# Four graph layers and an attention over one adjacency matrix: constants on another queue, the sixth sweep streamed and split, a third pair of score banks, and the last root by logarithm and exponential

## What is computed

```python
def ln(x): return (x - mean(x)) / sqrt(var(x) + 1e-5)          # over the 128 columns

# layer 0
inv_deg = 1 / (adj.sum(1) + beta)
x = ln(x + inv_deg[:, None] * (adj @ x + beta[:, None] * x) @ kernel + bias)
# layer 1: three products with adj, the first two 20 columns wide
h = relu(adj @ (x @ W1) + b1); h = relu(adj @ (h @ W2) + b2); h = relu(adj @ (h @ W3) + b3)
x = ln(x + relu(h + x))
# layer 2
d = 1 / (sqrt(adj.sum(1)) + 1e-8)
x = ln(x + (adj * d[:, None] * d[None, :]) @ (x @ W + b))
# layer 3: a product with adj, and an attention over all rows
B = softmax((x @ W_l) @ (x @ W_r).T) @ x
x = ln(x + adj @ x + gamma * (B @ W_h @ W_g))
```

## Time and profile before

| | us |
|---|---|
| median of 3 runs | 1466.33 (1464.1 to 1467.71) |
| the profiled execution | 1466.62 |
| its span, first to last instruction | 1464.8 |
| TensorE, VectorE, ScalarE, GpSimd busy in it | 1380.5, 900.9, 694.5, 235.7 |
| mean granted clock of TensorE | 0.994 |

### The profile page before, as it was taken

One profiled execution on the slowest core, in us unless ns is written; L12 is line 12 of the kernel. 1 busy time (PEld: TensorE's weight loads), 2 busy tenths in 40 slices (PEclk: granted clock), 3 DMA queues, 4 the chain that ended last, 5 costly groups with the idle time before them and its releaser, 6 DMA issues.

```text
span 1464.8 us, 17014 instructions
## 1 busy us (share of the span) xinstructions
PE 1380.5 (94%) x5831; PEld 789.8 (54%) x5831; DVE 900.9 (61%) x1223; ACT 694.5 (47%) x875; POOL 235.7 (16%) x136
## 2 busy tenths in 40 slices
PE   6999999988898899999999999999799999999995
PEld 2555555312122222257777777777567667767753
DVE  3676777300000022488888977776888888888875
ACT  1101011101010111176777866665687878788776
POOL 0111111000000000000101000002033334333343
PEclk9999999999999999999999999999999999999998
DMA  9876677799999999998989889883000000000001
GB/s 345 321 274 230 249 279 266 294 409 407 407 408 408 408 395 397 395 328 312 317 313 324 296 278 327 317 314 129 0 1 1 0 1 1 1 1 1 1 1 58
DMA packets 101151, 337.30 MB, mean 230 GB/s; under 512 B 11354, under 2 KB 12890, under 8 KB 101082
## 3 DMA queue, kind: packets, MB, share of 16 engines
q1 hardware_dynamic: 101082, 336.40, 61.5%
HBM read 334.26 MB, written 2.10 MB: 230 GB/s over the span
## 4 chain that ended last, share of the span: by engine, by line
PE 65%; DMA 13%; DVE 11%; ACT 5%; issue 3%; SPq 2%; POOL 0%; DVEq 0%; ACTq 0%
DMA raw<-in_adj_s 13%; PE acc L1076 11%; PE acc L1112 9%; PE acc L1173 6%; PE acc L1168 6%; PE acc L1169 6%; PE acc L1096 4%; PE acc L1196 4%; DVE peak L861 4%; PE acc L1261 3%; DVE ring L885 3%; ACT ring L615 2%; ACT ring L603 2%; DVE t_lo L794 2%; PE e L989 1%
## 5 line engine op out<-in xcount | busy, mean ns | idle before, releaser
L794 DVE TENSOR_TENSOR t_lo<-raw,t_hi 128x1024 fp32r<-128x1024 f32 x224 | 275.3, 1251 | 61.1 <-ACT t_hi L554 56.8
L554 ACT ACTIVATE t_hi<-raw 128x1024 fp32r<-128x1024 f32 x224 | 234.1, 1058 | 72.7 <-PE acc L1173 71.2
L1168 PE MATMUL acc<-t_hi,st_hi 128*128 128x512 f32 x448 | 201.7, 450 | 2.9 <-DVE st_lo L699 2.9
L475 POOL TENSOR_TENSOR ring_lo<-ring,p_hi 128x1024 fp32r<-128x1024 f32 x64 | 155.5, 2429 | 271.3 <-ACT p_hi L609 271.3
L1076 PE MATMUL acc<-raw,x 128*128 128x512 f32 x384 | 173.3, 606 | 14.6 <-DMA raw<-in_adj_s 14.6
L1112 PE MATMUL acc<-raw,h_a 128*20 128x512 f32 x736 | 162.5, 598 | 22.8 <-DMA raw<-in_adj_s 22.6
L1169 PE MATMUL acc<-t_hi,st_lo 128*128 128x512 f32 x448 | 175.3, 391 | 0.0
L725 DVE TENSOR_TENSOR xs<-e,bias 128x512 f32<-128x512 f32 x8 | 5.5, 690 | 267.0 <-PE e L992 267.0
L499 ACT ACTIVATE at<-acc 128x512 f32<-128x512 f32 x48 | 28.7, 597 | 289.4 <-PE acc L1112 180.9
L885 DVE TENSOR_TENSOR ring<-ring,e 128x1024 f32<-128x1024 f32 x128 | 154.2, 1210 | 0.1
L603 ACT ACTIVATE ring<-ring 128x1024 f32<-128x1024 f32 x128 | 134.7, 1054 | 36.9 <-DVE ring L885 36.8
(11 more groups left out here) (182 smaller groups left out, 2099.1 us busy)
## 6 DMA issues: line engine op xcount, KB each, us to landing
raw<-in_adj_s SPq DMA_DIRECT2D x584, 512.0 KB, 7.3
resident<-in_adj_s SPq DMA_DIRECT2D x16, 512.0 KB, 7.4
raw<-in_adj_s SPq DMA_DIRECT2D x24, 256.0 KB, 7.7
kept_t<-in_adj_s SPq DMA_DIRECT2D x8, 512.0 KB, 5.9
x<-in_x SPq DMA_DIRECT2D x4, 512.0 KB, 8.1
kept_s<-in_adj_s SPq DMA_DIRECT2D x8, 256.0 KB, 6.1
kept_v<-in_adj_s SPq DMA_DIRECT2D x8, 256.0 KB, 6.4
kept_l<-in_adj_s SPq DMA_DIRECT2D x8, 256.0 KB, 9.0
```

Of the source, the lines that this page charges most:

```text
L475: nc.gpsimd.tensor_tensor(ring_lo[:, n % RING, :], slot(n), p_hi[:, m % 2, :].bitcast(F32), ALU.subtract).then_inc(pl_done, 1)
L554: nc.scalar.activation(t_hi[:, (par * NS + g) % HL, :], raw[:, k, :], ACT.Copy).then_inc(hi_done, 1)
L794: nc.vector.tensor_tensor(t_lo[:, k, :], raw[:, slot_no(s, c, g), :], t_hi[:, k, :].bitcast(F32), ALU.subtract).then_inc(lo_done, 1)
L1168: mm(a[:, :], block_of(st_hi, b), hi[:, m], start=(b == 0), stop=False)
```

## The change

- *Constants.* The 18 loads leave SP's queue. ScalarE issues them once the last part of x is in, ahead of its copies of x.
- *Sweep 6* streams all 16 tiles, in 8 slots, and splits all; the resident blocks are not used in it. Its chunk ends are signalled by `pe_tile`.
- *Score banks.* The two accumulators become one tensor `acc01`, which serves as a third pair for the first 15 score steps.
- *Keys and added one.* `k_lo` goes from VectorE to GpSimd; from the fourth key chunk on, each is followed by one of the four additions. The split of the values is five steps later.
- *Peak row.* The four tensor_scalar and the f32 product give way to four transposes with `m4` broadcast as the stationary side.
- *Projection.* The row sums come first, with a semaphore of their own. VectorE's work for group 6 is seven steps later.
- *Last normalisation* in three parts. Blocks 0 to 15 and 16 to 23: variances, root and scales at steps 93 to 95 and 123 to 125, the norms on GpSimd behind its low parts. Blocks 24 to 31 after the last group, five on VectorE and three on ScalarE. The root and reciprocal are exp(-0.5 ln(v)).

```diff
-        LN_PARTS = ((0, NB - CB), (NB - CB, NB))
-        ACT_LN = {NT + 9: (0, 4), NT + 11: (4, 8), NT + 13: (8, 12), NT + 15: (12, 16)}
-        DVE_LN = {NT + 9: (16, 19), NT + 11: (19, 22), NT + 13: (22, 25), NT + 15: (25, 28)}
-        RESULT = ((0, 8, 1), (16, 22, 0), (8, 16, 1), (22, 28, 0), (28, 32, 0))
+        LN_PARTS = ((0, 16), (16, 24), (24, NB))
+        LN_SCALES = (NT - 34, NT - 4)
+        POOL_LN = {NT - 53: (0, 3), NT - 51: (3, 6), NT - 49: (6, 9), NT - 47: (9, 12), NT - 45: (12, 14), NT - 43: (14, 16),
+                   NT - 15: (16, 18), NT - 13: (18, 20), NT - 11: (20, 22), NT - 9: (22, 24)}
+        LN_LAST = (NB - 2 * CB, NB - 3, NB)
+        RESULT = ((0, 9, "fin_xp", 1), (9, 16, "fin_xp", 2), (16, 24, "fin_xp", 3), LN_LAST[:2] + ("fin_x", 1),
+                  LN_LAST[1:] + ("fin_xa", 1))
+        def score_bank(t):
+            return (rs01, e23, acc01)[t % 3] if t < KP - 1 else (e23, rs01)[t % 2]
...
@@ sync
-                        if g == RAW:
-                            for dst, src in consts:
-                                sp.dma_start(dst[:, :], src).then_inc(const_in, 16)
@@ gpsimd
+            def keys_lo(c):
+                pool.wait_ge(k_hi_done, c + 1)
+                nc.gpsimd.tensor_tensor(cols(k_lo, c - 1), cols(v, c), cols(k_hi, c - 1).bitcast(F32),
+                                        ALU.subtract).then_inc(k_lo_done, 1)
+            def normalise_first(a, b):
+                pool.wait_ge(fin_nmr, 1 if b <= LN_PARTS[0][1] else 2)
+                for n in range(a, b):
+                    i = nc.gpsimd.tensor_scalar(block_of(v, n), block_of(xf, n), rstd_a[:, n:n + 1],
+                                                nmr_a[:, n:n + 1], ALU.mult, ALU.add)
...
-            add_one()
+            pool.wait_ge(pe_tile, tile_no(S5, NC - 1, NG - 1) + 1)
+            pool.wait_ge(S["xb"], done("xb", 5, NC - 1))
+            for c in range(1, NC):
+                keys_lo(c)
+                if c >= NC // 2:
+                    add_one(c - NC // 2)
             for n in range(NT):
                 if n % KP in SPLIT:
                     weights_lo(n)
+                if n in POOL_LN:
+                    normalise_first(*POOL_LN[n])
@@ scalar
+            act.wait_ge(x_in[XP - 1], 16)
+            for dst, src in consts:
+                nc.scalar.dma_start(dst[:, :], src).then_inc(const_in, 16)
...
-                nc.scalar.activation(std_a[:, a:b], ve_a[:, a:b], ACT.Sqrt).then_inc(fin_std, 1)
+                nc.scalar.activation(std_a[:, a:b], ve_a[:, a:b], ACT.Ln).then_inc(fin_std, 1)
+                act.wait_ge(fin_std, part + 1)
+                nc.scalar.activation(rstd_a[:, a:b], std_a[:, a:b], ACT.Exp, scale=-0.5).then_inc(fin_rc, 1)
@@ vector
-                dve.wait_ge(m4_done, i + 1)
-                for b in range(CB):
-                    n = nc.vector.tensor_scalar(block_of(diag, b), ident[:, :], m4[:, b:b + 1], None, ALU.mult)
-                n.then_inc(diag_done, 1)
...
-                if i is not None and after == 2:
+                later = 7 if i == GQ - 2 else 0
+                if i is not None and after == 2 + later:
                     finish_sums(i)
@@ tensor
-                for g in range(NS):
-                    hi, lo = t_hi[:, (par * NS + g) % HL, :], t_lo[:, (par * NS + g) % HL, :]
+                for g in range(wide_tiles(s)):
+                    k = (par * wide_tiles(s) + g) % HL
+                    hi, lo = t_hi[:, k, :], t_lo[:, k, :]
...
+                    if s == S5:
+                        continue
                     if g in KEPT_AFTER and not first(c):
...
-                mm(free_banks[i % 2][:, :], ones_f[:, :], diag[:, :], start=True, stop=True).then_inc(row_mm, 1)
+                for b in range(CB):
+                    n = mm(block_of(free_banks[i % 2], b), m4[:, b:b + 1].broadcast_to([P, P]), ident[:, :],
+                           is_transpose=True, start=True, stop=True)
+                n.then_inc(row_mm, 1)
```

More of the change, by code:

```diff
@@ L29 @@
 NS = NG - RB // GB
+S4, S5 = 4, 5
 NT_N = 12
@@ L36 @@
 RAW = 8
-RAW_W = 7
+RAW_4 = 7
 HL = 4
@@ L406, in _ @@
             chunks(sp, step)
-            for n, (a, b, by_act) in enumerate(RESULT):
-                if by_act:
-                    sp.wait_ge(fin_xa, sum(r[2] for r in RESULT[:n]) + 1)
-                else:
-                    sp.wait_ge(fin_x, sum(not r[2] for r in RESULT[:n]) + 1)
+            for a, b, by, count in RESULT:
+                sp.wait_ge({"fin_x": fin_x, "fin_xa": fin_xa, "fin_xp": fin_xp}[by], count)
                 sp.dma_start(out[:, a * D:b * D], v[:, a * D:b * D]).then_inc(out_done, 16)
@@ L925, in last_scales @@
                 a, b = LN_PARTS[part]
-                dve.wait_ge(fin_std, part + 1)
-                nc.vector.reciprocal(rstd_a[:, a:b], std_a[:, a:b]).then_inc(fin_rc, 1)
                 dve.wait_ge(fin_rc, part + 1)
```

158 lines of the change are left out of this document (84 added, 74 removed).

## The result

The changed kernel takes 1441.47 us (median, 1440.11 to 1442.77) beside 1466.58 for the kernel before: a ratio of 0.9831, 95% interval [0.9814, 0.9848], 25.1 us less. The forecast was 1434, with a range of 1422 to 1447: the sign and the range held, and 7.5 of the 32.7 us forecast are missing. The profiled execution took 1440.11 us, its span 1438.5.

What follows compares the result with a forecast made beforehand. TensorE is busy 94% of the span, but each stage has its own limit. Terms 5.5 + 5.3 + 6 + 4 + 12.4 - 0.5 = 32.7 us off 1466.62 give 1434 us, range 1422 to 1447.

Steps and rivals of the forecast that it cites:

- Part 1: First chunk of sweep 1: constants on ScalarE's queue shorten TensorE's idle; 5.5 us gained, 3 to 7.5.
- after the shorter idle perhaps part of the 2.1: First chunk: of 2.1 us lost to TensorE running slow after its idle, part perhaps regained, within the 5.5 us.
- Rival (a): Start: constants late, bx comes after TensorE asks, first chunk gains 1 instead of 5.5 us; 1438 us; chance 8%.
- Part 2: Sweep 6: split products replace whole f32 ones, chunks go from 23.4 to 22.7 us; 5.3 us gained, 0 to 6.5.
- (c): Sweep 6: the stream tops out at 351 GB/s, so 67.1 MB take 191.2 us; 1441 us; chance 7%.
- (d): Sweep 6: slower kernel; at no more than 310 GB/s the sweep lasts 216.5 us, the point of no gain; chance 3%.
- Part 3: First sixteen score steps: third pair of banks and keys on GpSimd; 6 us gained, 2 to 9 by key subtraction cost.
- GpSimd paces: Score steps and drain: dearer GpSimd key subtractions and norms lose 3 us in each; 1440 us; chance 12%.
- Part 4: Peak row in seven groups outside the drain: transposes save TensorE 0.47 us each plus some waiting; 4 us gained, 1 to 7.
- Part 5: Drain after the last scores: norms leave ScalarE, 48.19 us becomes 35.8; 12.4 us gained, 9 to 14.
- hidden: Drain: GpSimd's two norm blocks in four step pairs, 0.70 us against 0.66 free, cost nothing; at 0.68 each 2.8 late.
- Part 6: Root and tail: tail 0.5 us longer, -0.3 to +2; table loads at the two earlier roots hidden.

Runs made afterwards that it cites:

- doubled norms: Changed kernel with every normalisation of blocks 16 to 23 on GpSimd made twice, the second result into a free buffer: 1446.81 us, 0.9867 of the kernel before.

## Why the prediction was right, point by point

**Part 1, constants.** The mechanism held, the term was too large: 5.5 against 3.15 alone. The 3.9 of the profiled execution are a good draw of a start that comes in at 44.6 on average, 2.9 less than before. Two steps failed. Tile 8 lands at 27 and not at 25 to 26.5, and "after the shorter idle perhaps part of the 2.1" came to 0.3. The cover of `bx` was 1 us: I had it ready at 31 to 36 from ScalarE's issues and copies, and left out that small loads behind megabytes of tiles take 13 us from issue to landing. Rival (a) came within 1 us of happening. The rule that I quoted from the Trainium skill ("DMA: Bandwidth & Descriptors", Issuing engines are not separate DMA queues) agrees with the kernel that issues the constants at once: another queue, and the tiles come later.

**Part 2, sweep 6.** 5.3 forecast, 6.5 measured, and 6.5 in the sweep when it is undone. Chunks of 22.6 to 22.76 came as said; the old ones are 23.51 to 23.66 and not 23.4, and the first two won 0.7 and 1.4 where I had put 0.3 and 0.7. Landing in 5.6 us stayed below the 7.9: rivals (c) and (d) didn't show.

**Part 3, third pair.** 6 forecast, 5.6 measured, 5.0 by undoing the banks. The hand-made schedule was near: steps 8, 10 and 14 start 13.8, 17.4 and 24.7 us after the first (14, 17.8, 25.5), with TensorE waiting for `k_lo`:

```profile
1022.91 0.50 PE L1252 MATMUL e<-q_hi,k_hi 128*128 128x512 f32 x1 [0.58 <-POOL k_lo L480]
```

GpSimd's prices were right, in groups by form:

```profile
L492 POOL TENSOR_SCALAR v<-xf,rstd_a,nmr_a 128x128 f32<-128x128 f32 x24 | 11.0, 472 | 5.5 <-DVE nmr_a L958 5.5
L485 POOL TENSOR_TENSOR x<-x,ones_f 128x1024 f32<-128x1024 f32 x4 | 9.6, 2397 | 0.0
L480 POOL TENSOR_TENSOR k_lo<-v,k_hi 128x512 fp32r<-128x512 f32 x7 | 9.0, 1289 | 22.4 <-ACT k_hi L632 22.4
```

1.29 for a key (1.22 taken), 2.40 for an addition (2.62). Of "GpSimd paces" the conclusion was too strong: without the additions in between, step 14 comes only 1.2 us sooner.

**Part 4, peak row.** A regular group lost 0.80, not 0.57, since four transposes take 0.44 in the chain and not the 0.66 of their record's modelled end, which I subtracted from 1.13. The larger slip is in the parts' borders: undone, the row costs 7.5 us by its stretches, because it also shortens the peak chain at the early root and in the drain, where one of the four tensor_scalar is held by GpSimd. About 2 of part 5's gain are the row's. Whether some of part 3's is, no run shows, since the clock fell there. The broadcast stationary brought no cost that shows.

**Part 5, drain.** Its length is right to half a microsecond, 35.3 against 35.8, with norms of 0.47 and not 0.35. But "hidden" hung on GpSimd's lead, as the waits behind the doubled norms show.

**Part 6, root and tail: the step that failed.** "The two earlier roots fall where ScalarE is busy 163.41 of 205.44 us; a table load there is hidden." Two loads in a row make the root 3.0 us, and ScalarE stands between a score and its maximum: the peak comes late at the group's end, 2.66 us once and 2.3 the second time. A mean idle share of a fifth says nothing on a stop of 3 us in a chain that has to be whole once a group. And which set is loaded was left to the rule: by the Trainium skill ("ScalarE: Activation LUTs", Table sets: the hidden batching unit) one set holds both functions; so it does, but this kernel as built takes another for each, and only the kernel that loads the common set by name shows the rule's count. By its stretches the loads are 6.3 us; the 5.3 of its median are what is left after the load's own place and the clock behind it took 1.5 back. The profiled execution missed by 6.4: these 6.3, 1.6 of part 1 and 0.4 of part 3, less 1.2 of sweep 6 and 0.7 in the rest. The range of 1422 to 1447 held by its width: part 6 was given -0.3 to +2, and the tail alone took 2.2, the stalls of the two early roots another 5.0. That the sum stayed inside is owed to the other parts, which came near the values taken.

## What to carry to other kernels

Before costing a switch of function on ScalarE at nothing, look whether the functions share a table set *and* whether that set is the one loaded; one load by name, early and out of the way, was worth more here than the rewrite of the root. An engine with idle time isn't a place to hide a stop of several microseconds if something waits for each of its results: ask what is due next behind it. Work given to GpSimd can hold any VectorE instruction that reads only SBUF in that time, so put it beside VectorE's work on PSUM. When several parts shorten the same chain, undo each alone; their gains don't add. And when two kernels differ in a stretch that the edit doesn't touch, or by more than a wait explains, read the granted clock there before looking for a cause.

## What the runs showed of the hardware

- A VectorE instruction with two SBUF operands doesn't run beside a GpSimd tensor_tensor; it ends just behind it: 0.41 became 1.91 and 2.58 us, 0.69 became 2.15, four of 1.25 became 7.25. In sweeps 5 and 6 of the changed kernel a subtraction beside GpSimd's copy takes 1.63 instead of 1.22, once a chunk. An instruction with one SBUF tensor was held too: a tensor_scalar of 128x128, 0.275 became 1.13 in the kernel before; a copy of 128x8, 0.17 became 0.79 in the drain of the changed kernel. One with an operand in PSUM wasn't held.
- GpSimd: a tensor_scalar of 128x128 with two scalars from memory 0.44 to 0.47 us, a tensor_tensor of 128x512 1.29, of 128x1024 2.40; 3.13 beside VectorE's subtractions in sweep 6.
- A table load took 1.283 us each time, with no pause behind it that shows: 1280.72 to 1283.54 holds two loads and a logarithm of 0.22.
- 18 small loads, 0.82 MB, issued on a second queue behind a full path, were complete 13 us after the last issue.
- Behind a wait of TensorE the granted clock fell to 0.50 in some executions and stayed at 1.00 in others: after 2.66 us, 1.00 in the changed kernel and 0.50 with sweep 6 undone, and the group is 53.2 us long in five kernels and 54.8 and 54.7 in two; after 1.94 us, 1.00 in the changed kernel and 0.50 with the peak row undone.
- Left open: why the clock falls behind one such wait and not behind its like.
